# Two transformer blocks on one core: the next query and key products stand behind the mixture's down products, directly in front of the next scores

## What is computed

```python
x = _layernorm(x + _L0_attn_ref(x, ...), axis=-1)  # RMS norm, 16 heads of 64, output projection, bias
x = _layernorm(x + _L0_ffn_ref(x, ...), axis=-1)   # shared expert + 8 experts (hidden 256), top 2 gates, gelu
x = _layernorm(x + _L1_attn_ref(x, ...), axis=-1)  # for each token, 16 heads of 8 attend to each other
x = _layernorm(x + _L1_ffn_ref(x, ...), axis=-1)   # 8 experts (hidden 512), top 2 gates, gelu
```

## Time and profile before

| | |
|---|---|
| median of 3 runs | 1415.86 us (1414.83 to 1416.04) |
| profiled execution, its own time | 1412.94 us |
| its span, first to last instruction | 1411.2 us |
| mean granted TensorE clock | 0.985 |
| busy: TensorE matmul, VectorE, ScalarE, GpSimd | 95%, 67%, 59%, 36% |
| one iteration (2 to 15) | 82.56 us |

### The profile page before, as it was taken

One profiled execution on the slowest core, in us unless ns is written; L12 is line 12 of the kernel. 1 busy time (PEld: TensorE's weight loads), 2 busy tenths in 40 slices (PEclk: granted clock), 3 DMA queues, 4 the chain that ended last, 5 costly groups with the idle time before them and its releaser, 6 DMA issues.

```text
span 1411.2 us, 33731 instructions
## 1 busy us (share of the span) xinstructions
PE 1336.5 (95%) x11200; PEld 1183.7 (84%) x11200; DVE 939.4 (67%) x2663; ACT 828.2 (59%) x2236; POOL 501.9 (36%) x410
## 2 busy tenths in 40 slices
PE   5787999999999999999999999999999999999767
PEld 4575888989898998989889898988989798898767
DVE  3347567576766757676676767767676776767684
ACT  4555565657556574765757476575747657564423
POOL 3306226070532607053260705326070531607100
PEclk9899999999999999999999999999999999999989
DMA  7100000000000000000000000000000000000000
GB/s 253 42 10 27 6 21 20 12 19 11 23 11 19 19 11 19 11 23 11 19 19 11 19 11 23 11 19 17 13 19 9 25 11 19 13 13 21 5 1 9
DMA packets 38528, 30.90 MB, mean 22 GB/s; under 512 B 9801, under 2 KB 37330, under 8 KB 38226
## 3 DMA queue, kind: packets, MB, share of 16 engines
q1 hardware_dynamic: 38194, 26.14, 6.4%
q10 hardware_dynamic: 288, 4.19, 0.8%
HBM read 27.94 MB, written 2.36 MB: 21 GB/s over the span
## 4 chain that ended last, share of the span: by engine, by line
PE 79%; issue 9%; DVE 3%; POOL 3%; POOLq 2%; DVEq 1%; DMA 1%; ACT 1%; SPq 0%; ACTq 0%
PE bank_F L1212 22%; PE bank_S L1094 7%; PE bank_A L1149 7%; PE bank_T L1127 7%; PE bank_T L1080 4%; PE bank_A L1140 3%; PE bank_T L1081 3%; PE bank_T L1082 3%; PE bank_A L1080 3%; PE bank_F L1080 3%; PE bank_F L1081 3%; PE bank_F L1082 3%; PE bank_A L1081 3%; PE bank_A L1082 3%; DVEq L350 1%
## 5 line engine op out<-in xcount | busy, mean ns | idle before, releaser
L1212 PE MATMUL bank_F<-down,hid 128*128 128x128 f32 x2944 | 356.0, 276 | 6.8 <-DVE x L803 6.1
L1212 PEld LDWEIGHTS bank_F<-down,hid 128*128 128x128 f32 x2944 | 340.4, 192 | 16.0 <-DVE x L803 9.6
L593 ACT ACTIVATE probs<-bank_S,neg_max 128x256 f32<-128x256 f32 x512 | 235.8, 475 | 167.4 <-DVE neg_max L720 167.4
L720 DVE TENSOR_REDUCE neg_max<-bank_S 128x2 f32<-128x512 f32 x256 | 164.5, 684 | 76.2 <-PE bank_S L1094 76.1
L516 POOL TENSOR_TENSOR hid<-hid,qkv 128x1024 f32<-128x1024 f32 x60 | 169.0, 2826 | 11.3 <-ACT hid L609 11.3
L577 ACT ACTIVATE probsT<-bank_T 128x512 f32<-128x512 f32 x256 | 139.0, 601 | 51.3 <-PE bank_T L1127 51.2
L803 DVE SCALAR_TENSOR_TENSOR x<-bank_F,gates,x 128x128 f32<-128x128 f32 x496 | 149.5, 343 | 28.7 <-PE bank_F L1212 20.1
L486 POOL TENSOR_TENSOR mean_sq<-sum_sq,one_over_d 128x2 f32<-128x2 f32 x16 | 3.1, 195 | 433.7 <-ACT h_row L572 433.7
L1149 PE MATMUL bank_A<-probsT,values 128*64 128x256 f32 x1024 | 139.8, 394 | 7.7 <-DVE hid L737 4.4
L504 POOL TENSOR_TENSOR hid<-qkv 128x1024 f32<-128x1024 f32 x45 | 121.0, 2689 | 59.3 <-ACT qkv L577 59.3
L1127 PE MATMUL bank_T<-ident,probs 128*128 128x128 f32 x1024 | 139.3, 279 | 0.1
(11 more groups left out here) (184 smaller groups left out, 2998.5 us busy)
## 6 DMA issues: line engine op xcount, KB each, us to landing
inv_spread<-sums_apart SPq DMA_DIRECT2D x256, 64.0 KB, 2.6
sums_apart<-sum_invT SPq DMA_DIRECT2D x512, 0.5 KB
x_row<-in_x SPq DMA_DIRECT2D x16, 128.0 KB, 2.2
hid<-in_w ACTq DMA_DIRECT2D x1, 2048.0 KB, 8.2
down<-in_w ACTq DMA_DIRECT2D x1, 2048.0 KB, 13.8
out<-x SPq DMA_DIRECT2D x16, 128.0 KB, 1.9
hid<-in_rw SPq DMA_DIRECT2D x1, 1024.0 KB, 7.7
hid<-in_wv SPq DMA_DIRECT2D x1, 512.0 KB, 3.9
```

The costliest lines, as they stand in the source:

```text
L593: ins = sc.activation(probs[:, h // 2 % 2, h % 2, t, :], unit.bank(f"S{h}")[:, t * S:(t + 1) * S], ACT.Exp, bias=neg_max[:, h, t:t + 1], a ...
L720: ve.tensor_reduce(neg_max[:, h, :], v.bank(f"S{h}")[:, :].rearrange("p (t k) -> p t k", t=NT), AX.X, ALU.max, negate=True).then_inc(max_r ...
L1212: ins = te.matmul(bank[:, (j * NT + t) * P:(j * NT + t + 1) * P], hid[:, e, k, tokens(t)], down[:, e, k, :], start=k == 0, stop=k == m - 1)
```

## The change

In each attention step the unit QK(s+3) is put on TensorE's list behind the fillers of place 1 instead of in front of them. In step s that makes T(2s), T(2s+1), [filler], QK(s+3), and then S(2s+4), S(2s+5) of step s+1. Only the list moves; the other engines' programs, the rings and the number of units stay. HT stands in step 6, where there is no QK.

```diff
         put("F", *fill_units(it, s, 0))
         put("T0", f"T{2 * s}", on=a)
         put("T1", f"T{2 * s + 1}", on=a)
-        put("A", f"QK{s + 3}", on=a and s + 3 < HP)
         put("A", "HT", on=nxt and s == HP - 2)
         put("F", *fill_units(it, s, 1))
+        put("A", f"QK{s + 3}", on=a and s + 3 < HP)
     put("A", f"O{HP - 1}", "OUT", on=a)
```

## The result

The changed kernel takes 1430.40 us in the median of 4 runs (1428.64 to 1431.47), the kernel before 1415.34 in 4 runs (1413.76 to 1416.04). The ratio is 1.011 (95% interval 1.0097 to 1.0122): slower by 15 us, where the prediction said slower by 7 and its range ended at 1428. The sign and the place in step 1 were right. Half of the loss came from a second place, which the prediction had looked at and priced at nothing.

What follows compares the result with a forecast made beforehand. TensorE's unbroken matmul stream was taken as the bound. 0.70 - 0.19 - 0.05 = 0.46 us, times 14, plus 0.70 for iteration 1, made 7.1 us over 1415.86: forecast 1423.0 us, range 1417.5 to 1428.

Steps and rivals of the forecast that it cites:

- the one repeated wait before D0p3: TensorE, step 1, iterations 1 to 15: 0.24 us of idling until VectorE has mixed D0p2, which held bank F0.
- Neighbours: Steps 0 and 2, T to the next S: new order sums to the same 3.52 us, cost 0, within 0.05 a step.
- Step 1: QK4 behind D0p3 leaves the wait for D0p2's mix bare: T to S 4.69 us against 3.99, loss 0.70.
- Step 4: QK7 behind D1e1 no longer waits for its bank: T to S 3.52 us against 3.71, gain 0.19.
- Step 3: QK6 behind LQ0 and LQ1: 0.05 us gained, bounds 0.10 gained and 0.15 lost, if X2T's copy clears LQ0.
- Other engines: Later ScalarE copies of QK and of LQ0/LQ1, feeding GpSimd, are covered by 1.95 and 0.81 us of idling: cost 0.
- The clock: TensorE's stop of over 1.1 us once an iteration keeps the full clock: no cost; rival that it falls, 1475, chance 0.02.
- More: step 3 loses: Rival: LQ0 waits for X2T and GpSimd comes late, another 0.2 to 0.4 us an iteration, 1426 to 1429; chance 0.12.
- Faster: Rival: D0p3's wait isn't VectorE's, so steps 3 and 4 still pay, 1412.5, down to 1409 us; chance 0.04.
- no change: Rival: slack later in the iteration gives the loss back, about 1416 to 1418 us; chance 0.07.

Runs made afterwards that it cites:

- the changed kernel with LQ first: Changed kernel, but in step 3 ScalarE copies LQ0 and LQ1 out ahead of QK6; ratio 1.0113 to the kernel before.
- the runs with LQ0 first: ScalarE copies LQ0 and LQ1 out ahead of QK6, on the changed kernel (ratio 1.0113) and on the kernel before (1.0067).

## Why the prediction was right and wrong

- *Bound by TensorE's stream; the one repeated wait before D0p3.* Right, but it was not the only repeated one: O6's 0.12 us stood in the same 0.36 us of idling, and I took note of its size alone, not of who ended it.
- *Neighbours, 0 a step.* Right: 3.52 us before and after in step 0.
- *Step 1, 0.70 us.* Right: 0.71, and 0.97 us of idling in place of 0.24. D0p3 starts 0.06 us behind the mix (608.93 + 1.28 = 610.21). The run with QK4 alone gives 1.0082 where 1.0074 was worked out.
- *Step 4, 0.19 us gained.* Right for TensorE, wrong for the time: the run with QK7 alone is at 0.9993. The sum booked it as a gain at the end, without asking what sets the end between step 4 and O6.
- *Step 3, 0.05 us gained.* 0 measured. X2T's copy did clear LQ0 by D1e0's earlier end, as said: it ends at 622.78 + 0.38 = 623.16, and LQ0 starts at 623.21, 0.89 us behind T. LQ0 to QK6 takes 1.10 us where 1.21 was worked out, but QK6 to S takes 625.39 - 624.31 = 1.08 where I put 0.88. This contact stood nowhere in the trace of before, and I had built it from two others.
- *Other engines, "both cost 0".* **This is the step that failed.** Its size was right (LQ0 handed on up to 0.65 us later against what follows; it was 0.65), and the cover was not one. I read GpSimd's 0.81 us of idling before its fourth product as slack. But the exp that ends this idling follows L844, and L844 ends 0.27 to 0.29 us behind GpSimd's own add. The idling is therefore 0.81 us however late GpSimd is: it is 0.81 in the changed kernel too, with the same releaser, and in the runs with QK4, QK6 or QK7 alone. A wait whose end moves with the waiter's own start is no slack. The price came out on VectorE, and 1.2 + 0.6 + 0.4 us of its work later on O6. It was 0.66 us an iteration, 14 x 0.66 = 9 us; the forecast of the loss, 7 us, fell short of the 15 by 8.
- *The clock.* No cost, right: 1.00 in the whole iteration after a stop of 0.97 us.
- *The rivals.* "More: step 3 loses" had the right source (GpSimd comes late) at a chance of 0.12, with 1426 to 1429; its mechanism, by way of X2T and the layer norm behind OUT, was not what happened. "Faster" fell with the 0.06 us between mix and D0p3, "no change" with the longer iteration; its sentence that GpSimd's chain moves with TensorE is wrong too, for the chain moved by 0.65 us against the scores.

0.71 + 0.66 - 0.19 = 1.18 us an iteration against 0.46 forecast.

The rule that was missed is written in the Trainium skill, "SBUF — State Buffer", Who interferes with whom: a VectorE instruction with two inputs in SBUF contends with a GpSimd instruction that reads SBUF, and the one that comes first keeps the other out for the whole instruction. The traces agree: L844 0.43 us alone and 1.43 beside the add; L814 1.36 us where it met the last 0.28 us of GpSimd's add (619.51 + 1.28 against 620.51 in the kernel before), 1.80 where it met the last 0.72 (kernel after), 3.07 and 3.19 where GpSimd's product had begun. By the same section reductions do not contend on this chip. The traces agree with this as well: the second sum of L839, which reads SBUF, takes 0.69 us in the kernel after with GpSimd's product running throughout (636.40 to 637.09, the product to 637.39) and 0.69 in the changed kernel with LQ first, where GpSimd rests for three quarters of it (636.51 to 637.20, the add to 636.69). By that rule the change had to be followed to every operation of two SBUF operands on VectorE during GpSimd's six.

## What to carry to other kernels

When a change moves the start of a chain on GpSimd, in either direction, go through VectorE's operations with two SBUF operands that fall beside it, and look whether their lengths differ between otherwise equal instances (L844 was 0.43 and 0.78 us in one iteration already): a varying length of the same shape is a hidden wait. An idle bracket is slack only if what ends it does not itself hang on the waiting engine. And where a move lays a wait bare, look at what it makes ready sooner: with QK3 and QK4 alone moved and the mix put where its input now is, 8 us came off; QK4 alone without it cost 12.

## What I had not expected of the hardware

- GpSimd's time of one operation can hide the wait from the other side. L504 takes 2.35 to 2.39 us, but the one that L814 precedes takes 3.33 to 3.36; L511 took 2.07 in place of 1.28 when L814 was let in before it (both in the runs with LQ0 first).
- Of three starts of GpSimd's chain the middle one is the best, within less than 1 us: 0.5 us earlier cost 0.67%, 0.4 later 0.55%, in a kernel where GpSimd is busy 36% of the time.
- The time from the first T of iteration 15 to the end is 156.3 to 157.8 us in the eight profiled executions whose granted clock was 1.00 in its first 60 us, and 159.1 to 159.8 in the four where it was 0.94 to 0.97. What sets it there was not tried.
